# More descriptor room for GpSimd's indirect transfers, and two one-column buffers given up for it

## The chip, the cores and the metric

The kernel runs on one core of a Trainium2 chip. The metric is device time in microseconds (us) of one execution.
## The reference

One transformer layer on x of 1 x 2048 x 256, all in float32:

```python
x = x + layernorm(attention(layernorm(x)))   # 16 heads of 128, weights = 4-bit codes * block scales
x = x + layernorm(moe(layernorm(x)))
# moe: 8 experts, the two best of each token, weights from a softmax over the logits
combine = top-2 of softmax(x @ Wr), normalised
h = silu(x @ Wg[e]) * (x @ Wu[e]);  y = sum over e of combine[e] * (h @ Wd[e])
```

## The kernel before

Attention takes the first 1850 us. It works in 128 steps (`HALVES`: 16 heads of 8 slices of 256 queries), and every engine follows an order written out by hand. Values that need full precision are split into a high and a low part, so that each product is three matmuls (`product3`, lines 620 to 624).

The expert stage follows, and the change touches it. The 2048 tokens are 16 tiles of 128 rows, in two parts of 8 (`PART_TILES`). Each part is handled so:

1. PE turns the normed rows (`turn_rows`) and computes the router's logits (`route`, lines 842 to 857). DVE picks each token's two experts and works out the row that the token gets in a table sorted by expert (`shift_logits` to `rows_of`); the last step writes `row` (line 1756), an int32 index per token and choice. `seat_experts` then writes `expert_i` (line 1767), the expert of each seat. A seat is 128 rows of the table for one expert; part 0 and part 1 have 23 seats each (`SEATS`), 46 in all (`NS`).
2. POOL's `send(u)` (lines 587 to 596) scatters the tiles into the table `x_rows[u]` in DRAM: two indirect DMAs for each tile, one per choice, 16 for a part, each of 128 rows of 1 KB. All 16 of a part count on one semaphore, `x_sent[u]`.
3. SP's `load_seat` (lines 446 to 453) waits at seat 0 and at seat 23 until all 16 scatters of that part have landed, and loads each seat into one of four `xg` buffers. Before seat j it waits until seat j - 4 has been turned.
4. PE handles the seats in one order: `turn_h(n - 2)`, `turn_x(n + 1)`, `gate_up(n)`, `down(n - 3)` (lines 969 to 979). Its matmuls take the expert's weights at an address from a register; `expert_of` (lines 895 to 903) loads the register from `expert_i`. Seats 0 to 10 have theirs loaded ahead of part 1's rows; those of seats 11 to 22 are loaded in one run of 12 between `route(1)` and `turn_x(0)` (lines 965 to 968). ACT and DVE split the results (`seat_hi`, `seat_lo`, `gate`, `hidden`, `hidden_hi`, `hidden_lo`), and ACT empties the down product (`seat_out`, line 1276). The two turned tiles are signalled by `xg_t` (for ACT and SP) and `h_t` (for ACT).
5. `store_seat` writes each result to `y_rows[u]`; POOL's `fetch(t)` (lines 598 to 608) gathers each token's two rows by indirect DMA once the part's stores have landed, into four `yg` buffers with one semaphore each, and ACT and DVE weigh, add, norm and add the residual.

POOL's order in this stage is `down_lo`, `send(0)`, `send(1)`, `fetch(0..15)`. `send(1)` waits for part 1's `row`, which DVE computes while the first seats run.

`zero` (line 78) is one column of zeros, a bias operand for ACT in `scale_row` and `weigh` (lines 1123 and 1283); `warm` (line 85) takes the result of one square root whose only use is to have ACT load that table early (line 1190). `zeros` (128 x 256) is the source with which SP clears `x_rows` (line 434), and `wr_raw` holds the router's weights until POOL has split them at the start (lines 487 to 491).

Of the kernel before, what the change touches and what calls it, by code (L numbers as in the profile page):

```python
# [8 lines left out]
def sandwich_layer(nc, x, wq, sq, bq, wk, sk, bk, wv, sv, bv, wo, so, bo, wr, wg, wu, wd, out):  # L9
# [6 lines left out]
    f32, f32r = mybir.dt.float32, mybir.dt.float32r  # L16
    ALU, ACT, AX = mybir.AluOpType, mybir.ActivationFunctionType, mybir.AxisListType

    P = 128
# [26 lines left out]
    BATCHES = [(0, 8), (8, 4), (12, 4)]  # L46
    DVE_FROM = [6, 4]
    SEATS = [2 * n + E - 1 for _, n in PART_TILES]
    FIRST_SEAT = [sum(SEATS[:u]) for u in range(PARTS)]
    NS = sum(SEATS)  # L50
# [16 lines left out]
    with ctx:  # L67
        ctx.enter_context(nc.allow_non_contiguous_dma(reason="per-head bias columns"))

        def sem(name):  # L70
            return ctx.enter_context(nc.semaphore(name))

        def sb(name, shape, dt, stack=ctx):
            return stack.enter_context(nc.sbuf_tensor(name, shape, dt))

        ident = sb("ident", [P, P], f32)
        zero = sb("zero", [P, 1], f32)
        xT_hi = sb("xT_hi", [P, DC, S], f32r)
        xT_lo = sb("xT_lo", [P, DC, S], f32r)  # L80
        acc = sb("acc", [P, TT, D], f32)
        stats = sb("stats", [P, TT, 6], f32)
        mv = sb("mv", [P, TT, 2], f32)
        std = sb("std", [P, TT], f32)
        warm = sb("warm", [P, 1], f32)
        base = sb("base", [P, TT], f32)
        zeros = sb("zeros", [P, D], f32)
        wr_raw = sb("wr_raw", [P, DC, E], f32)
        wr_both = sb("wr_both", [P, DC, 2, E], f32r)
        rstd = sb("rstd", [P, TT], f32)  # L90
        shifted = sb("shifted", [P, TT], f32)
# [144 lines left out]
        sm = {n: sem(n) for n in names}  # L236
# [46 lines left out]
        def live(w):  # L283

            return 0 <= w < HALVES
# [29 lines left out]
        def bias_head(n):  # L315

            h, s = divmod(n, NH)
            if s == 3 and h == H - 2:
                return H - 2
            return (H - 1 if h == H - 2 else h) if s == 5 and 0 <= h < H - 1 else None  # L320
# [157 lines left out]

        @block.gpsimd
        def _(pool):  # L480
            pool.memset(zero[:, :], 0.0).then_inc(sm["ident_set"], 1)
            pool.memset(ident[:, :], 0.0).then_inc(sm["ident_set"], 1)
            pool.wait_ge(sm["ident_set"], 2)
            pool.affine_select(out=ident[:, :], in_=ident[:, :], compare_op=ALU.not_equal, fill=1.0,
                               base=0, pattern=[[-1, P]], channel_multiplier=1).then_inc(sm["ident_ready"], 1)

# [45 lines left out]
            for k, h in (("q", 0), ("v", 0), ("v", 1)):  # L532
                weights(k, h, first_codes[f"{k}{h}"], first_scales[f"{k}{h}"])

            pool.memset(zeros[:, :], 0.0).then_inc(sm["zeros_set"], 1)

            def constants():

# [444 lines left out]
        def _(act):  # L983
# [38 lines left out]
            def exps(w, r, g):  # L1022

                if not live(w):
                    return
                s = w % NH
                wait(act, "shift_ready", RH * w + r + 1)

                if r == 0 and g == 0:
                    wait(act, pT_loaded[s % 2], LOADS * (w // 2))  # L1030
                    if w == 0:
                        act.wait_ge(w_ready["q"], 1)
                        act.wait_ge(w_ready["v"], 2)
                out = blocks(s, g)[:, :, :, r, :].rearrange("p j t q -> p t j q")
                src = ring_of("s", w, NG2 * r + g).rearrange("p (t j q) -> p t j q", t=GT, j=Q4)
                if w == LAST:
                    out, src = natural(w)[:, r, g, :], ring_of("s", w, NG2 * r + g)
                nc.scalar.activation(out, src, ACT.Exp, bias=shift[:, s % SLOTS, r:r + 1],  # L1038
                                     scale=SCALE, accum_out=sums[:, s % SLOTS, r, g:g + 1])\
                    .then_inc(sm["p_ready"], 1)  # L1040

            def probs_hi(w, p):

                if not live(w):
                    return
                s, g, t = w % NH, p // GP, 2 * (p % GP)
                if p == 0 and w != LAST:
                    wait(act, pT_loaded[s % 2], LOADS * (w // 2 + 1))

                wait(act, "pv_done", PAIRS_KT * w + p - RING + 1)  # L1050
                if w == LAST:
                    wait(act, "last_turned", p // 2 + 1)
                    nc.scalar.activation(pT_hi[:, p, :], turned_pair(p), ACT.Copy).then_inc(sm["p_hi_done"], 1)
                    return
                nc.scalar.activation(pT_hi[:, p, :].rearrange("p (i n) -> p i n", i=Q4),  # L1055
                                     pT[:, s % 2, :, g, t:t + 2, :].rearrange("p i t q -> p i (t q)"),
                                     ACT.Copy).then_inc(sm["p_hi_done"], 1)

            def out_hi(w):

                if not live(w):
                    return
                s = w % NH
                wait(act, "pv_done", PAIRS_KT * (w + 1))

                wait(act, "oproj_ready", w)
                if w == LAST:
                    nc.scalar.activation(oT_hi[:, :], ps_a[:, s % 2, 0:HQ], ACT.Copy).then_inc(sm["out_hi"], 1)
                    return
                nc.scalar.activation(oT_hi[:, :].rearrange("p (r i q) -> p i r q", r=RH, i=Q4),  # L1070
                                     ps_a[:, s % 2, 0:HQ].rearrange("p (i r q) -> p i r q", r=RH, i=Q4), ACT.Copy)\
                    .then_inc(sm["out_hi"], 1)

            def q_hi(w):

                if not live(w):
                    return
                h, s = divmod(w, NH)
                wait(act, "q_ready", w + 1)
                if bias_head(w - 2) is not None:  # L1080
                    wait(act, "vb_ready", bias_head(w - 2) + 1)
                nc.scalar.activation(qT_hi[:, s % 2, :], ps_a[:, (s + 1) % 2, 0:HQ], ACT.Identity,
                                     bias=bias_all["q"][:, h:h + 1]).then_inc(sm["q_hi"], 1)

            def k_hi(h, b):
                wait(act, "k_ready", 2 * h + b + 1)
                cols = slice(b * HALF, (b + 1) * HALF)
                nc.scalar.activation(kT_hi[:, cols], ring_of("k", h, b), ACT.Identity,  # L1088
                                     bias=bias_all["k"][:, h:h + 1]).then_inc(sm["k_hi"], 1)

            def value_hi(pair, u):
                wait(act, "v_ready", VU * pair + u + 1)
                wait(act, "pv_done", PAIRS_KT * (2 * NH * pair - 1) + VT // 2 * (u + 1))
                nc.scalar.activation(v_hi[:, :, u * VT:(u + 1) * VT, :].rearrange("p e a d -> p a e d"),
                                     ring_of("v", pair, u).rearrange("p (a e d) -> p a e d", a=VT, e=2), ACT.Copy)\
                    .then_inc(sm["v_hi_done"], 1)

            def bias_hi(h):
                wait(act, "vb_ready", h)
                nc.scalar.activation(vb_hi[:, :], ident[:, :], ACT.Identity, bias=bias_all["v"][:, h:h + 1], scale=0.0)\  # L1100
                    .then_inc(sm["vb_hi_done"], 1)
# [58 lines left out]
            for n in range(-1, HALVES):  # L1160
                h, s = divmod(n, NH)
                inner, new_pair = live(n), live(n) and h % 2 == 0
                if n < 0:
                    q_hi(0)
                if bias_head(n + 1) is not None:
                    bias_hi(bias_head(n + 1))
                if new_pair and s == 3:
                    value_hi(h // 2, 2)
                probs_hi(n - 2, 1)
                exps(n, 0, 0)  # L1170
                if new_pair and s == 3:
                    value_hi(h // 2, 3)
                probs_hi(n - 2, 2)
                exps(n, 0, 1)
                if n >= 0:
                    q_hi(n + 1)
                probs_hi(n - 2, 3)
                probs_hi(n - 2, 4)
                probs_hi(n - 2, 5)
                probs_hi(n - 2, 6)  # L1180
                exps(n, 1, 0)
                exps(n, 1, 1)
                if new_pair and s in (1, 2):
                    value_hi(h // 2, s - 1)
                out_hi(n - 3)
                if s == NH - 1 and h + 1 < H:
                    k_hi(h + 1, 0)
                probs_hi(n - 2, 7)
                if n == LAST:
                    nc.scalar.activation(warm[:, :], zero[:, :], ACT.Sqrt).then_inc(sm["warm_done"], 1)  # L1190
                probs_hi(n - 1, 0)
                if s == NH - 1 and h + 1 < H:
                    k_hi(h + 1, 1)
# [739 lines left out]
```

## Time and profile before

| | |
|---|---|
| median of 3 runs | 2086.07 us (2084.23 to 2086.74) |
| the profiled execution | 2085.8 us |
| its span, first to last instruction | 2084.1 us |
| outside the span | 1.7 us |
| PE busy in the span | 1971.1 us, 95% |
| expert stage, from `send(0)` to the end | 1876.8 to 2084.1 us |

Sum what a change does inside the span; the 1.7 us around it stay. PE's share is an average: the attention is bound by PE, and the expert stage, which holds all indirect transfers, has stretches in which PE waits. The views with times are those to read for them: the chain of work that ended last, followed back from the end, the timelines of single engines, and the instructions of one line. Times in them are us from the span's start.

### The profile page before, as it was taken

Reading aid. Unit: us, or ns where it says so; the run is one execution under the profiler, and the core shown is the slowest. Engines: PE = TensorE matmul, PEld = TensorE weight load, DVE = VectorE, ACT = ScalarE, POOL = GpSimd, SP = SyncE. Lnnn points to the kernel's source line nnn. Section 1 sums busy time; section 2 is a strip of 40 time slices with the busy share of each in tenths; the row PEclk is TensorE's granted clock in tenths of the full one; section 3 lists DMA queues with packets and bytes.
Section 4 is the critical chain, followed back from the end, with each engine's and each line's share of the span. In section 5 each row is a group of like instructions: output and inputs, shape, how many; then the busy total and the mean of one; then the engine's idle time right before and its main releaser. Section 6 shows DMA issues by size and latency. Waiting matters only on the chain.

```text
span 2084.1 us, 33186 instructions
## 1 busy us (share of the span) xinstructions
PE 1971.1 (95%) x10902; PEld 1703.5 (82%) x10902; DVE 1750.8 (84%) x2706; ACT 1418.9 (68%) x2686; POOL 1528.5 (73%) x1317
## 2 busy tenths in 40 slices
PE   7999999999999999999999999999999999976882
PEld 5888888888888888888888888888888888865772
DVE  6889889998989888988999898988898888975344
ACT  4777767776777767776777677776777677763444
POOL 2679778887779777977888777977797787974222
PEclk9999999999999999999999999999999999987886
DMA  4667767786678667775777666766677576832343
GB/s 98 159 156 185 177 142 177 172 192 150 165 163 190 158 151 163 179 162 136 163 165 175 147 152 156 179 151 144 155 177 167 135 165 147 210 92 92 115 127 104
DMA packets 173040, 322.66 MB, mean 155 GB/s; under 512 B 47686, under 2 KB 105798, under 8 KB 172870
## 3 DMA queue, kind: packets, MB, share of 16 engines
q1 hardware_dynamic: 169798, 312.15, 64.0%
q0 software_dynamic: 3072, 8.39, 1.3%
q8 instruction: 89, 1.46, 0.3%
q14 instruction: 81, 0.66, 0.1%
HBM read 35.68 MB, written 18.35 MB: 26 GB/s over the span
## 4 chain that ended last, share of the span: by engine, by line
PE 82%; SPq 4%; POOL 3%; ACT 3%; DVE 3%; issue 2%; DMA 1%; another core or an unknown queue 1%; POOLq 0%; ACTq 0%
PE ps_a L750 20%; PE ps_s L622 14%; PE ps_s L624 13%; PE ps_s L623 13%; PE ps_a L751 10%; PE ps_a L622 3%; SPq L396 3%; PE ps_a L624 3%; PE ps_a L623 3%; POOL pT_both L519 2%; ACT probs L1038 1%; DVE part_max L1394 1%; POOL x_rows L595 1%; PE ps_s L928 1%
## 5 line engine op out<-in xcount | busy, mean ns | idle before, releaser
L519 POOL TENSOR_TENSOR pT_both<-pT,pT_both 128x512 fp32r<-128x512 f32 x1016 | 1291.2, 1301 | 339.9 <-ACT pT_both L1055 337.8
L1038 ACT ACTIVATE probs<-ps_s,shift 128x1024 f32<-128x1024 f32 x512 | 566.6, 1110 | 275.6 <-DVE shift L1403 275.5
L750 PE MATMUL ps_a<-pT_both,v_both 128*128 128x512 f32 x2048 | 744.3, 397 | 0.7 <-POOL pT_both L519 0.5
L1055 ACT ACTIVATE pT_both<-pT 128x512 fp32r<-128x512 f32 x1016 | 606.7, 629 | 162.8 <-DMA pT<-probs 128.8
L1419 DVE STREAM_TRANSPOSE probs<-probs 128x1024 f32<-128x1024 f32 x508 | 614.5, 1229 | 56.8 <-ACT probs L1038 55.9
L1394 DVE TENSOR_REDUCE part_max<-ps_s 128x1 f32<-128x1024 f32 x512 | 612.5, 1215 | 20.6 <-PE ps_s L624 19.0
L751 PE MATMUL ps_a<-pT_both,v_both 128*128 128x256 f32 x2048 | 573.9, 280 | 0.0
L750 PEld LDWEIGHTS ps_a<-pT_both,v_both 128*128 128x128 f32 x2048 | 385.5, 188 | 86.1 <-POOL pT_both L519 1.3
L622 PE MATMUL ps_s<-kT_hi,qT_hi 128*128 128x512 f32 x1024 | 406.6, 397 | 11.7 <-ACT probs L1038 8.6
L623 PE MATMUL ps_s<-kT_lo,qT_hi 128*128 128x512 f32 x1024 | 403.3, 394 | 0.0
L624 PE MATMUL ps_s<-kT_hi,qT_lo 128*128 128x512 f32 x1024 | 401.9, 392 | 0.0
L751 PEld LDWEIGHTS ps_a<-pT_both,v_both 128*128 128x128 f32 x2048 | 386.7, 189 | 15.9
L622 PEld LDWEIGHTS ps_s<-kT_hi,qT_hi 128*128 128x128 f32 x1024 | 192.4, 188 | 56.9 <-ACT probs L1038 10.4
L624 PEld LDWEIGHTS ps_s<-kT_hi,qT_lo 128*128 128x128 f32 x1024 | 192.6, 188 | 45.1
L623 PEld LDWEIGHTS ps_s<-kT_lo,qT_hi 128*128 128x128 f32 x1024 | 192.8, 188 | 22.5
L1476 DVE SCALAR_TENSOR_TENSOR acc<-ps_a,rinv,acc 128x256 f32<-128x256 f32 x240 | 104.0, 475 | 2.4 <-PE ps_a L624 2.2
L606 POOL DMA_INDIRECT yg<-y_rows,row x32 | 31.1, 972 | 96.7 <-DMA y_rows<-y_sb 74.8
L1038 ACT ACTIVATION_READ_ACCUMULATOR probs<-ps_s,shift 128x1 f32 x512 | 98.8, 193 | 0.0
L1491 DVE SCALAR_TENSOR_TENSOR kT_lo<-ps_s,bias_k,kT_hi 128x1024 fp32r<-128x1024 f32 x32 | 41.1, 1284 | 43.7 <-ACT kT_hi L1088 43.7
L622 PE MATMUL ps_a<-w_o_hi,oT_hi 128*128 128x256 f32 x256 | 73.6, 288 | 1.2 <-DVE oT_lo L1439 1.2
L622 PE MATMUL ps_a<-xT_hi,w_q_hi 128*128 128x256 f32 x256 | 72.4, 283 | 0.0
L623 PE MATMUL ps_a<-w_o_lo,oT_hi 128*128 128x256 f32 x256 | 72.2, 282 | 0.0
(202 smaller groups left out, 2596.6 us busy)
## 6 DMA issues: line engine op xcount, KB each, us to landing
pT<-probs SPq DMA_DIRECT2D x2032, 128.0 KB, 2.3
x_rows<-zeros SPq DMA_DIRECT2D x46, 128.0 KB, 2.1
xg<-x_rows SPq DMA_DIRECT2D x46, 128.0 KB
y_rows<-y_sb SPq DMA_DIRECT2D x46, 128.0 KB
pT<-in_L_attn_x SPq DMA_DIRECT2D x4, 512.0 KB, 5.6
codes<-in_L_attn_wk_codes SPq DMA_DIRECT2D x16, 128.0 KB, 2.4
scales<-in_L_attn_wk_scales SPq DMA_DIRECT2D x64, 32.0 KB, 2.9
codes<-in_L_attn_wo_codes SPq DMA_DIRECT2D x16, 128.0 KB, 2.3
```

What stands on the lines that cost most here:

```text
L396: sp.dma_start(dst, src).then_inc(pT_loaded[s % 2], 16)
L519: pool.tensor_tensor(pT_lo[:, p, :].rearrange("p (i n) -> p i n", i=Q4), pT[:, s % 2, :, g, t:t + 2, :].rearrange("p i t q -> p i (t q)"), ...
L622: nc.tensor.matmul(dst, lhs_hi, rhs_hi, start=first, stop=False)
L623: nc.tensor.matmul(dst, lhs_hi, rhs_lo, start=False, stop=False)
L624: return nc.tensor.matmul(dst, lhs_lo, rhs_hi, start=False, stop=last)
L750: nc.tensor.matmul(out_both, v_hi[:, h % 2, k, :], move, start=k == 0, stop=False)
L751: last = nc.tensor.matmul(out, v_lo[:, h % 2, k, :], move[:, 0], start=False, stop=k == KT - 1)
L1038: nc.scalar.activation(out, src, ACT.Exp, bias=shift[:, s % SLOTS, r:r + 1], scale=SCALE, accum_out=sums[:, s % SLOTS, r, g:g + 1])\
L1055: nc.scalar.activation(pT_hi[:, p, :].rearrange("p (i n) -> p i n", i=Q4), pT[:, s % 2, :, g, t:t + 2, :].rearrange("p i t q -> p i (t q)" ...
L1394: V.tensor_reduce(part_max[:, s % SLOTS, r, g:g + 1], ring_of("s", w, NG2 * r + g), AX.X, ALU.max)\
L1419: V.transpose(tile, tile).then_inc(sm["p_turned"], 1)
L1476: ins = V.scalar_tensor_tensor(acc[:, t, :], part, scale, acc[:, t, :], ALU.mult, ALU.add)
```

## The change

The scratch area for indirect transfers grows from 1024 to 4096 bytes per partition. To pay for it, `zero` and `warm` lose their own buffers: `zero` becomes the first column of `zeros`, `warm` the first column of `wr_raw`. The fill of `zeros` moves from behind the first weights to the very start of POOL's program, in the place of the fill of `zero`, and the wait ahead of the `affine_select` counts one fill in place of two. Each buffer takes a multiple of 32 bytes of a partition, so 64 are given back and those above the two lie 3008 bytes higher.

```diff
-        zero = sb("zero", [P, 1], f32)
...
-        warm = sb("warm", [P, 1], f32)
         base = sb("base", [P, TT], f32)
         zeros = sb("zeros", [P, D], f32)
+        zero = zeros[:, 0:1]
         wr_raw = sb("wr_raw", [P, DC, E], f32)
+        warm = wr_raw[:, 0, 0:1]
...
-            pool.memset(zero[:, :], 0.0).then_inc(sm["ident_set"], 1)
+            pool.memset(zeros[:, :], 0.0).then_inc(sm["zeros_set"], 1)
             pool.memset(ident[:, :], 0.0).then_inc(sm["ident_set"], 1)
-            pool.wait_ge(sm["ident_set"], 2)
+            pool.wait_ge(sm["ident_set"], 1)
...
-            pool.memset(zeros[:, :], 0.0).then_inc(sm["zeros_set"], 1)
...
-                    nc.scalar.activation(warm[:, :], zero[:, :], ACT.Sqrt).then_inc(sm["warm_done"], 1)
+                    nc.scalar.activation(warm, zero[:, :], ACT.Sqrt).then_inc(sm["warm_done"], 1)
...
-    nc = bacc.Bacc("TRN2", target_bir_lowering=False, num_devices=1, dynamic_dma_scratch_size=1024)
+    nc = bacc.Bacc("TRN2", target_bir_lowering=False, num_devices=1, dynamic_dma_scratch_size=4096)
```

## Rows read from the trace of the kernel before

**Rows 1.** The page: its first line.
```profile
span 2084.1 us, 33186 instructions
```

**Rows 2.** POOL's timeline: start us, us, operation, [idle before <-releaser].
```profile
1876.79 1.20 POOL L595 DMA_INDIRECT x_rows<-acc,row  x1 [8.30 <-issue]
...
1888.18 0.97 POOL L595 DMA_INDIRECT x_rows<-acc,row  x1 [2.03 <-issue]
...
1898.88 0.97 POOL L595 DMA_INDIRECT x_rows<-acc,row  x1 [2.04 <-issue]
...
1922.49 0.96 POOL L595 DMA_INDIRECT x_rows<-acc,row  x1 [20.86 <-DVE row L1756]
...
1933.10 0.96 POOL L595 DMA_INDIRECT x_rows<-acc,row  x1 [2.04 <-issue]
```

**Rows 3.** POOL's and ACT's timelines while part 0's results are gathered.
```profile
1987.57 0.98 POOL L606 DMA_INDIRECT yg<-y_rows,row  x1 [41.63 <-DMA y_rows<-y_sb]
...
1996.40 0.95 POOL L606 DMA_INDIRECT yg<-y_rows,row  x1 [0.30 <-issue]
...
1997.66 0.32 ACT L1260 ACTIVATE silu_g<-ps_a 128x176 f32<-128x176 f32 x1 [3.64 <-remote]
```

**Rows 4.** The chain that ended last, in order: start us, us, what.
```profile
1886.14 2.03 issue
...
1896.84 2.04 issue
...
1900.16 3.01 DMA x_rows<-acc,row
1903.19 2.06 DMA xg<-x_rows
1905.29 0.70 PE ps_s L891 x2
```

**Rows 5.** Line 903, 1890 to 1906: ns min/median/max, first and last start.
```profile
L903 PEldq TENSOR_LOAD <-expert_i x12: 295/301/552, 1895.7 to 1903.1; - x12
...
L903 PEldq SEQ_ASSERT  x12: 18/18/18, 1896.3 to 1903.7; - x12
```

**Rows 6.** DVE's timeline, its work for part 1's routing.
```profile
1898.37 0.29 DVE L1666 TENSOR_REDUCE logits<-ps_s 128x64 f32<-128x128 f32 x1 [3.04 <-PE ps_s L855]
...
1903.12 0.28 DVE L1707 TENSOR_TENSOR which<-rank,count 128x128 f32<-128x128 f32 x1
```

**Rows 7.** What SP's queue waited for from 1895 on: us, times, longest.
```profile
SPq L453 <- DMA x_rows<-acc,row: 63.7, 1, 63.7
```

**Rows 8.** The timeline of PE and ACT during part 1's scatters.
```profile
1924.34 0.41 PE L622 MATMUL ps_a<-gu_hi,xs_hi 128*128 x1
...
1926.74 0.41 PE L622 MATMUL ps_a<-gu_hi,xs_hi 128*128 x1
...
1931.13 0.38 ACT L1268 ACTIVATE hs_hi<-ps_s 88x256 fp32r<-88x256 f32 x1 [3.95 <-remote]
...
1935.62 0.64 PE L622 MATMUL ps_a<-gu_hi,xs_hi 128*128 x1
...
1939.25 0.40 PE L622 MATMUL ps_a<-gu_hi,xs_hi 128*128 x1
...
1946.26 0.64 PE L622 MATMUL ps_a<-gu_hi,xs_hi 128*128 x1
...
1949.71 0.41 PE L622 MATMUL ps_a<-gu_hi,xs_hi 128*128 x1
```

**Rows 9.** The start: POOL's fills, PE's warm-up and its first real work.
```profile
0.80 0.10 POOL L481 MEMSET zero<- 128x1 f32 x1 [0.29 <-POOLq L1922]
...
1.62 7.21 PE L639 MATMUL ps_a<-ident 128*128 128x128 f32 x40 [1.62 <-POOL ident L484]
...
10.90 1.09 PE L633 MATMUL ps_s<-ident,pT 128*128 128x128 f32 x8 [2.07 <-ACT pT L1001]
...
21.61 0.31 POOL L535 MEMSET zeros<- 128x256 f32 x1
```

## The prediction

> **What bounds the kernel now.** I read the chain of waits first, from the end back to the start of the expert stage, because only what stands in it can shorten the run. Around POOL's first 16 scatters it runs through POOL alone: send by send, then the landing of the last scatter, the load of seat 0 (1903.19 to 1905.25), and PE's first turn of a seat at 1905.29 [rows 4]. Among the sends it has two pieces called "issue" of 2.03 and 2.04 us [rows 4]. POOL's timeline shows where they lie: ahead of the 8th and the 15th send, where all others of this run follow after 0.30 us, as in the gathers [rows 2, 3]. In part 1 the same stands ahead of the 8th and the 15th of its sends (the 24th of all, at 1933.10, and the 31st likewise) [rows 2]. So after every seven sends in a row comes one wait. The count began anew after the pause of 20.86 us ahead of the 17th send [rows 2]: the 17th to the 23rd went freely, the 24th waited. That is the picture of a room that holds seven transfers and is full when the eighth comes. Each wait ends about 2.05 us after POOL is through with the send before it, which is also what the load of seat 0 took to land [rows 4]: POOL waits for the newest of the seven, not for the oldest, which was sent over 10 us before. The gathers, up to eight in a row, never waited (0.30 us ahead of the eighth) [rows 3]. They differ in that each pair has its own semaphore, where the 16 scatters of a part share one; so the room of an old pair can be taken back alone.
>
> **The room, four times as large.** By scale it holds 28 transfers. The waits at sends 8, 15 and 24 find no reason any more. The first send that could meet a full room is the 29th, the 13th of part 1, and what it has to take back first are part 0's, which had all landed by 1903.19 [rows 4]. I take all four waits as gone; should one in part 1 stay, it costs 1.74 us of POOL's time with nobody behind it, as shown below. Each wait is 2.03 or 2.04 us less the usual 0.30, so the two of part 0 give 1.73 + 1.74 = 3.47 us: the last scatter lands at 1899.7, and seat 0 is there at 1905.25 - 3.47 = 1901.78.
>
> **What is late next.** PE doesn't stand idle until then. Between `route(1)` and `turn_x(0)` its queue loads 12 experts' numbers, one after the other: the first load starts at 1895.7, the last assert at 1903.7, which is 8.0 / 12 = 0.67 us for each [rows 5]. They depend on nothing that moves, so `turn_x(0)` can't start before 1903.72. I put it at 1903.75: a gain of 1905.29 - 1903.75 = **1.54 us**, and the remaining 1.93 us of the 3.47 are hidden. The other candidate is DVE, which must be through with `choose(1)` before `seat_lo(0)`: its last piece starts at 1903.12 and takes 0.28, end 1903.40 [rows 6]. The seat's low part would be wanted some 1.1 us after the turn starts (two turns 0.70 [rows 4], one ACT copy 0.38 as in [rows 8]), at 1904.8. DVE is free by then. The bounds of this term are 0 (the loads are slowed and end where the data came before) and 3.47 (they end early). The Trainium skill, page "DMA: Bandwidth & Descriptors", section "Latency and other measured facts", gives a floor of some 600 ns for such a register load. The trace has 0.67 us for one with its two register operations; by the page's figure, estimated, 12 would end at 1895.7 + 7.2 = 1902.9, and the term would be 2.4 us. The row decides.
>
> **Part 1's scatters** end 3.47 us earlier too, but SP's queue waited for a scatter once only, at seat 0 [rows 7]; seat 23, the first of part 1, is loaded long after they have landed. The gathers wait for stores of results, not for sends. Price of the direct effect: 0.
>
> **The indirect effect on the seats.** While POOL issues, PE's signals reach ACT late: in part 1's run ACT sat idle 3.95 us with its input turned, put down to "remote", which no engine of one core can be [rows 8]. The first matmul of `gate_up` came every 1926.74 - 1924.34 = 2.40 us before, and then at 1935.62, 1939.25, 1946.26 and 1949.71 [rows 8]. Four seats in 22.97 us, where 9.6 would do: 13.4 us are lost during and just behind part 1's scatters, 8.9 - 2.4 = 6.5 on the first of them and 7.0 - 2.4 = 4.6 on the third. The 13.4 us don't come from the waits for room as such, since ACT also lost 3.64 us while POOL gathered without a wait [rows 3]. After the change POOL issues 16 sends in one run of about 16 x 1.27 = 20.3 us (0.97 + 0.30 for one [rows 2]) in place of 7, 7 and 2 with two breaks. I take the loss as unchanged, 0, between two ends: it falls by the third seat's 4.6 us plus the seat behind it, 3.45 - 2.40 = 1.05, so by 5.65; or it grows by 7.2 us (rival 2). That is the widest term, and no row settles it.
>
> **The edits with one answer.** The fill of 256 columns takes 0.31 us where that of one took 0.10 [rows 9], and stands ahead of `ident`: PE's warm-up starts and ends up to 0.21 us later, at 9.04 in place of 8.83, and PE's first real work starts at 10.90 on ACT's norm [rows 9]. Price 0, hidden by that; 0.21 us if the cover were gone. The old fill at 21.61 goes [rows 9]; it frees 0.31 us of POOL that nobody waits for, at most a gain of the same size. `warm` and `zero` at other addresses take the same instructions and no new wait, on ACT's queue too. All other buffers shift by 3008 or 3040 bytes; no row prices that, and I bound it by 0.2 us either way, the size of the fill's edit.
>
> **Sum.** 2084.1 - 1.54 = 2082.6 us of span, with 1.7 us outside it 2084.3 for a profiled execution [rows 1]. That execution (2085.8) lay 0.27 us below the median of 2086.07, so the prediction in terms of the median is 2086.07 - 1.54 = **2084.5 us**.
>
> **The rivals.**
>
> 1. *The loads don't bind.* If PE's loads end earlier once POOL disturbs them less, the whole 3.47 us come through, less what DVE takes: its 1903.40 against 1901.78 + 1.1 = 1902.9 costs 0.5, so 3.0 us: 2083.1. Against it: their end is in the trace [rows 5], with POOL idle ahead of it for 2.04 us.
> 2. *One long run starves the seats (slower).* Place: PE's signals to ACT and SP in part 1's run. The breaks of 2 us are what lets them through: ACT's late piece started at 1931.13, when POOL had just finished its seventh send and was waiting until 1933.10 [rows 2, 8]. Without a break the seat in flight would stand still until the 16 sends are through, some 20.3 us after the start. PE began three seats between 1926.74 and 1946.26 [rows 8]; all three, 3 x 2.4 = 7.2 us of work, would come behind the run. Time: 2084.5 + 7.2 = 2091.7. A milder form has the loss grow with the time that POOL issues, with 14 sends x 1.27 = 17.8 us before, 13.4 x 20.3 / 17.8 = 15.3, so +1.9: 2086.4. It decides from the point where more than 1.54 us are added. Against it: gathers without a break let ACT go on too, if late.
> 3. *One long run has one stall.* If each run stalls once, the second goes: 2084.5 - 5.65 = 2078.9. For it: the loss came once in each of the two long runs [rows 8].
> 4. *The waits aren't for room.* They could be POOL held up by DVE's work, and then stay whatever the room: 2086.1. But DVE was idle for 3.04 us until 1898.37, through most of the second gap, which began at 1896.84 [rows 4, 6], and the strict count of seven speaks for room. That such a hold exists is what the Trainium skill says (page "SBUF — State Buffer", section "SBUF: two separate sides": GpSimd can't write descriptors while VectorE has the port that they share); here the trace doesn't show it.
>
> **How the numbers follow.** The forecast (1.54 us, the seats' loss as before or within 2 us of it) 0.45; rival 1 0.10; rival 2 0.22, of which 0.12 above 2090.2; rival 3 0.15; rival 4 0.08. The range from 2079.0 to 2090.0 takes in rival 3 but for half of its lower side, and rival 2 up to three quarters of its price; what is left out is some 0.2. A measurement tells about 0.2%, 4.2 us, from no change. Faster than 2081.9 is rival 3 and a little of rival 1 and of the forecast with a smaller loss: 0.20. Slower than 2090.2: 0.12. The rest, 0.68, is within 0.2%.
>
> **What would show it.** In POOL's timeline, 0.30 us ahead of every scatter but the 1st and 17th. Seat 0's load landing some 1.9 us before PE's turn of it, and that turn starting right behind the last assert of line 903, about 8 us after the first load. The spacing of `gate_up` from the 8th seat on tells rivals 2 and 3. The prediction is wrong if the gaps of 2 us stay, if the turn starts well before or after that assert, or if the seats during part 1's scatters lose much more or less than 13 us.

## The result

In the sitting in which the change was judged (a sitting is one chip with the kernel before timed beside the others), the kernel before has a median of 2084.09 us and the changed kernel 2088.89 us: a ratio of 1.0024, 95% interval 1.0014 to 1.0034, so **slower by 4.8 us** where 1.5 us faster was predicted. The profiled execution has 2090.6 us of span. Later sittings were of two kinds, and this is the larger finding: where the kernel before has 2085 us the changed one has 1.0027 (1.0016 to 1.0038); where it has 2063 us, the changed one has **0.9975** (0.9966 to 0.9985), faster by 5.3 us. Ratios compare executions in the fast state; one of 11 of the kernel called `spaced` below took 6843 us and stands in none of them.

The waits for room are gone, as said. POOL's timeline of the changed kernel, with the lines that answer to those of [rows 2], has 0.30 us ahead of the 8th send (1883.33) and of the last; all that follow between them are alike:

```profile
1883.33 0.96 POOL L594 DMA_INDIRECT x_rows<-acc,row  x1 [0.30 <-issue]
...
1893.44 0.96 POOL L594 DMA_INDIRECT x_rows<-acc,row  x1 [0.30 <-issue]
```

The chain of waits (start, us, what) shows what came in their place. Before, it ran through POOL's sends and the load of seat 0 [rows 4]. Now it doesn't touch them:

```profile
1890.34 0.60 ACT xT_hi L1148
1890.93 2.19 another core or an unknown queue
...
1893.14 0.60 ACT xT_hi L1148
1893.74 2.92 another core or an unknown queue
...
1896.68 0.60 ACT xT_hi L1148
...
1898.65 0.38 PE ps_s L852
...
1902.02 0.21 PE ps_s L854
1902.23 4.26 issue
1906.49 0.70 PE ps_s L890 x2
```

PE has turned part 1's rows, but the signals of two of the four turns reach ACT 2.19 and 2.92 us after ACT is ready. One core has no other core to wait for; this is the piece that [rows 8] called "remote". The 32 matmuls of `route(1)` behind them (lines 852 and 854) stand 0.21 us apart, at a granted clock of 0.50; from 1893.80 to 1897.60 in the profile of before they ran at 0.89, in 3.85 us in place of 7.27. The row of line 902's loads shows how the delay goes on: they start three microseconds later than in [rows 5], 5.8 us later if counted from the first send, and PE's turn of seat 0 (1906.49) stands right behind the last assert.

```profile
L902 PEldq TENSOR_LOAD <-expert_i x12: 295/301/307, 1898.7 to 1905.9; - x12
...
L902 PEldq SEQ_ASSERT  x12: 18/18/18, 1899.3 to 1906.4; - x12
```

In part 1's run the same thing is larger. ACT's timeline has idle times of 3.99, 7.12 and 5.36 us; PE's has the seats:

```profile
1932.29 0.38 ACT L1267 ACTIVATE hs_hi<-ps_s 88x256 fp32r<-88x256 f32 x1 [3.99 <-remote]
...
1940.75 0.32 ACT L1259 ACTIVATE silu_g<-ps_a 128x176 f32<-128x176 f32 x1 [7.12 <-remote]
1946.43 0.38 ACT L1267 ACTIVATE hs_hi<-ps_s 88x256 fp32r<-88x256 f32 x1 [5.36 <-remote]
```

```profile
1927.94 0.41 PE L621 MATMUL ps_a<-gu_hi,xs_hi 128*128 x1
...
1936.03 0.64 PE L621 MATMUL ps_a<-gu_hi,xs_hi 128*128 x1
...
1949.74 0.64 PE L621 MATMUL ps_a<-gu_hi,xs_hi 128*128 x1
```

Between the ninth `gate_up` and the eleventh lie 21.8 us; in [rows 8] two steps from 1926.74 take 12.5. I use four numbers of each profiled execution from here on: the **first send**; **gate 0**, from the first send to the first matmul of `gate_up`; **early loss**, from `gate_up` of seat 0 to that of seat 22, less 22 x 2.40; and **late loss**, the same for the 23 steps behind it, in which part 0's results are gathered. The two profiles of the judged sitting:

| kernel | span | first send | gate 0 | early loss | late loss |
|---|---|---|---|---|---|
| before | 2084.1 | 1876.79 | 30.5 | 13.5 | 13.1 |
| changed | 2090.6 | 1873.99 | 34.5 | 17.5 | 14.1 |

So 4.0 us are lost ahead of the seats, 4.0 in part 1's run, 1.0 in the gathers and 0.3 behind the last seat; and 2.8 come back from ahead of the first send, which nothing in the prediction allowed.

### The profile page after: what moved, and what is told of

The parts are those of the page before. It is cut to its first block, busy times and chain, and to the rows that moved or that the text cites. A ratio compares the mean times of both kernels' runs of the same rounds, so it can differ in the third digit from the quotient of the medians.

```text
span 2090.6 us, 33185 instructions
## 1 busy us (share of the span) xinstructions
PE 1968.6 (94%) x10902; PEld 1700.9 (81%) x10902; DVE 1752.0 (84%) x2706; ACT 1417.8 (68%) x2686; POOL 1524.8 (73%) x1316
## 4 chain that ended last, share of the span: by engine, by line
PE 75%; SPq 6%; POOL 5%; DVE 5%; ACT 4%; issue 2%; DMA 2%; another core or an unknown queue 1%; POOLq 0%; ACTq 0%; DVEq 0%
PE ps_a L749 18%; PE ps_s L621 13%; PE ps_s L622 12%; PE ps_s L623 12%; PE ps_a L750 9%; SPq L396 6%; POOL pT_both L519 4%; PE ps_a L621 3%; PE ps_a L623 3%; PE ps_a L622 3%; ACT probs L1037 2%; DVE part_max L1393 1%; DMA pT<-probs 1%; DVE probs L1418 1%
## 5 line engine op out<-in xcount | busy, mean ns | idle before, releaser
L621 PE MATMUL ps_s<-kT_hi,qT_hi 128*128 128x512 f32 x1024 | 406.6, 397 | 11.7 <-ACT probs L1037 8.6
L605 POOL DMA_INDIRECT yg<-y_rows,row x32 | 30.4, 951 | 106.2 <-DMA y_rows<-y_sb 84.1
```

The lines of the kernel that those rows point to most:

```text
L621: nc.tensor.matmul(dst, lhs_hi, rhs_hi, start=first, stop=False)
```

## The experiments

Three theories. **A**: PE's signals are late while POOL issues indirect transfers without a pause; the waits for room were pauses. **B**: the traffic of the scattered rows holds them up. **C**: the small edits cost it.

**The edits alone.** The room back at 1024, all other edits kept.

```
-dynamic_dma_scratch_size=4096
+dynamic_dma_scratch_size=1024
```

> The changed kernel with its room put back to 1024 bytes; the edits to the zero column, the warm-up scratch and the start of POOL stay. Theory (the longer runs of scatters hold up PE's signals; part 0: turn_x(0) came 32.50 us after the first send where it came 28.50 us after it before, part 1: the four slowed steps of the seats 26.9 us where they were 23.0): the waits of 2.03 us are back at the 8th, 15th, 24th and 31st send, turn_x(0) 28.5 us behind the first send, and the time is that of before, ratio 0.999 to 1.001. Rival (the small edits cost it: the attention moved, or the code): no wait changes that, 1.002 or more. Third: the profile of after began its first send 2.80 us earlier than before; if that comes from the edits and not from scatter of the runs, this one is at 0.9987.

Measured: 0.9988 (0.9977 to 0.9999), before at 2084.36. Gate 0 is 30.5, the early loss 11.9, as before. C falls with its sign turned: the edits *win* about 2.5 us (0.2 to 4.8 by the interval). The profiles show where. `v_proj` issues groups of 24 matmuls of 128x256 on w_v. First and last of one group, before:

```profile
515.04 0.28 PE L622 MATMUL ps_s<-w_v_hi,xT_hi 128*128 128x256 f32 x1
...
517.76 0.28 PE L624 MATMUL ps_s<-w_v_hi,xT_lo 128*128 128x256 f32 x1
```

and in the changed kernel:

```profile
514.03 0.28 PE L621 MATMUL ps_s<-w_v_hi,xT_hi 128*128 128x256 f32 x1
...
516.64 0.28 PE L623 MATMUL ps_s<-w_v_hi,xT_lo 128*128 128x256 f32 x1
```

2.72 us against 2.61 for 23 steps: 118.3 and 113.5 ns for one. In two profiles of before all whole groups of the 32 have 117.8 to 118.7. In three profiles of kernels with the edits the first of every four has 117.4 to 117.8 and the other three 113.5 to 113.9, but for the second and third of all, which lie between. The granted clock is 1.00 around both groups shown. The three products have 256 such matmuls each, so 768 / 24 = 32 groups; three quarters of them x 0.11 = some **2.6 us**. No instruction changed; the addresses did. That this is the cause is argued, and which buffer's address counts wasn't tried.

**Which of the waits mattered.** Both kernels have the room of 28. POOL stops ahead of a part's 8th and 15th send until those out have landed, in part 0 alone or in part 1 alone.

```
 for k in range(2):
+    sent = 2 * (t - PART_TILES[u][0]) + k
+    if u in (0,) and sent in (7, 14):      # (1,) in the other
+        pool.wait_ge(x_sent[u], 16 * sent)
```

> The changed kernel, with its room of 28 transfers, and in part 0 alone POOL waits for the transfers that are out before the 8th and the 15th send; part 1's run stays unbroken. Theory: it is the stop in POOL's run that lets PE's signals through, so turn_x(0) is again 28.5 us (27.0 to 29.5) behind the first send and the 4.0 us of part 0 come back, while part 1 keeps its loss of about 3.9 us: ratio about 1.0005 to 1.001 against before (after minus 4.0 is 2084.9, with the scatter of the profile 2085 to 2087). Rival (the size of the room matters itself, or the loss sits in part 1 alone): 1.0024 stays, 2089.

> The changed kernel, with its room of 28 transfers, and in part 1 alone POOL waits for the transfers that are out before its 8th and 15th send; part 0's run stays unbroken. Theory: turn_x(0) stays 32.5 us behind the first send (31 to 33), the gate_up steps from the ninth to the thirteenth take 23.0 us again instead of 26.9, ratio about 1.0005 to 1.001 (2085 to 2087). Rival (all the loss is in part 0): 1.0024 stays, 2089. Should both this and the kernel with part 0's waits give the 4.9 us nearly alone, then neither loss simply adds up.

Measured, in the sitting of the kernel with the edits alone (0.9988) and against before: part 0's waits 1.0025 (1.0012 to 1.0038), gate 0 30.8, early loss 18.2. Part 1's waits 1.0001 (0.9991 to 1.0010), gate 0 31.2, early loss 9.3. I had expected each to bring half. ACT's timeline with part 1's waits has pieces put down to "remote" only up to the first pause (POOL's second run starts at 1929.11):

```profile
1926.64 0.38 ACT L1267 ACTIVATE hs_hi<-ps_s 88x256 fp32r<-88x256 f32 x1 [3.25 <-remote]
1927.37 0.38 ACT L1251 ACTIVATE xs_hi<-ps_s 128x256 fp32r<-128x256 f32 x1 [0.34 <-remote]
1928.88 0.32 ACT L1259 ACTIVATE silu_g<-ps_a 128x176 f32<-128x176 f32 x1 [0.85 <-remote]
```

The seats behind it are still slowed, with steps of 3.5, 3.8 and 4.8 us, but the piece of 7.12 us is gone. Most of the change's loss sits in part 1's run, and a wait in that run had kept it small. The larger room by itself isn't what makes the early loss: it is 28 here too, with 9.3 us.

**Pauses that wait for seats.** In part 1 each pair of sends waits for ACT's signal of a seat.

```
+if u == 1:
+    pool.wait_ge(sm["xs_hi_done"], 8 + 3 * (t - PART_TILES[1][0]) // 2)
```

> The changed kernel; part 0's run unbroken, and in part 1 each pair of sends waits for seats: pair i (0 to 7) for the 8 + 3i/2-th signal of xs_hi (ACT), so that two sends of 2.53 us together come every 3.6 us with about 1 us free between them, and the last one about seat 18, ahead of seat 20 at which SP first asks for them. Theory (a signal of PE comes late only while POOL issues one indirect transfer straight after another, and only some us into such a run, 2 to 5): the seats keep their 2.40 us through part 1's sends, the 13 us that before lost there and the 17 of after vanish: 2089 - 17 = 2072, down to half that gain if pairs still disturb, 2080. Rival 1 (each indirect transfer holds up signals, however far apart): the same loss spread over more seats, 2089. Rival 2 (part 1's seats then wait for their rows at seat 23): the idle time shows ahead of PE's turn of x at seat 23 on a DMA, 2080 to 2092.

Measured: 0.9996 (0.9985 to 1.0007), early loss 10.7; a miss. The waits of two neighbouring seats let four sends go in a row, four times, and each run of four, 4.7 us long, cost 2.1 to 3.3 us, with ACT idle on "remote" for 1.01, 2.61, 2.61 and 3.50 us.

**The next sitting: nothing is late.** Four kernels were meant to measure the length of the run and the cause.

```
room14, the room alone:
+dynamic_dma_scratch_size=2048
single1, ahead of each send of part 1:
+pool.wait_ge(sm["xs_hi_done"], 8 + 2 * (t - PART_TILES[1][0]) + k)
pair1, ahead of each pair of part 1:
+pool.wait_ge(sm["xs_hi_done"], 8 + 2 * (t - PART_TILES[1][0]))
plain1, in place of each send of part 1 (it leaves out the sorting by expert:
the rows lie in the order of the tiles, so part 1's results are others):
+pool.dma_start(x_rows[1][n * P:(n + 1) * P, :], acc[:, t, :]).then_inc(x_sent[u], 16)
```

> The changed kernel with a room of 2048 bytes (14 transfers by the count seen at 1024). POOL should stop 2.04 us only ahead of the 15th and the 31st send. Theory as it stands after the first four kernels (the loss sits in part 1's run and grows with the length of the unbroken run; seats 0 to 22 lost 9.3 to 13.5 us against a pace of 2.40 us where part 1's sends went 7, 7, 2 and 17.5 to 18.2 us where they went 16 in a row): a run of 14 loses nearly as much as one of 16, 15 to 18 us, ratio 1.001 to 1.002. Rival (only what a run has beyond some 10 sends is dear, or a few microseconds of stop anywhere free the signals): 10 to 13 us, ratio about 0.999 to 1.000.

> The changed kernel; part 0's run unbroken, part 1's sends one for each seat: send i (0 to 15) waits for the (8 + i)-th signal of xs_hi (ACT), so that 1.26 us of issue stand in every 2.40 us, with about 1.1 us free after each. In the kernel with waits for each pair the pairs of neighbouring seats had joined to four runs of four, and each of these cost 2.1 to 3.3 us. Theory A (PE's signal is late only when POOL issues without a pause): no seat is slowed by the sends, seats 8 to 19 at 2.40 us, loss over seats 0 to 22 about 1 to 2 us from other causes. Theory B (each indirect transfer or each start of a run costs something): 16 times 0.6 us or more, 10 us and up. In either case the last send goes at seat 22 only, and seat 23 waits for its rows, 3 to 7 us by the DMA rows (landing 3.0, load 2.1): ratio 0.998 by A, 1.002 by B.

> The changed kernel; part 0's run unbroken, part 1's sends two for every second seat: pair i (0 to 7) waits for the (8 + 2i)-th signal of xs_hi (ACT), 2.53 us of issue in every 4.80 us, with 2.2 us free behind each pair. Theory A (late only in an unbroken run, from its second or third microsecond on): a run of two is over before a signal is held up, or one in some is: loss over seats 0 to 22 at most 4 us. Theory B (every start of a run costs 2 to 3 us, as each run of four did): 8 x 2.5 = 20 us. Seat 23 waits for its rows as with single sends, 2 to 6 us: ratio 0.998 to 0.999 by A, over 1.004 by B.

> The changed kernel, but part 1's 16 scatters are 16 ordinary transfers of the same 128 rows of 1 KB to fixed places of the same array, issued by POOL at the same point (the rows then lie in the order of the tiles and not by expert: that part of the result is another). Theory (it is POOL's own work on an indirect transfer, 0.96 us of it for each, that holds up PE's signals): seats 8 to 12 keep 2.40 us, the loss over seats 0 to 22 falls from 17.5 to 1 or 2 us, the span to 2090.6 - 16 = 2074 or less. Rival (it is the traffic of the scattered rows in the 16 DMA queues, the signal waiting behind it): the same bytes go in less time, so the loss stays above 5 us and may come at once and longer.

Before was at 2061.44, 23 us faster than until then. Ratios 0.9977 (0.9966 to 0.9987), 0.9993 (0.9984 to 1.0002), 0.9996 (0.9987 to 1.0005); plain1 had one execution, 2058.9. Early losses 0.4, 3.5, 2.8 and 0.4, late losses 1.2 to 2.6. Even a run of 14 sends lost nothing, so these four don't tell A from B at all. They do say that the room counts as the prediction had it: with 2048 bytes POOL stops 2.12 us ahead of the 15th send and 2.43 ahead of the 31st. The 3 us of single1 and pair1 are seat 23 waiting for its rows, 3.04 us on "DMA xg<-x_rows" in single1.

**Again, beside both kernels.**

> The kernel before once more, for its profile beside those of this call. Until here the kernel before had 2084 us in two sittings, with seats slowed by 12 to 13 us during part 1's scatters and again during part 0's gathers, and 2061 us in a third, in which no kernel showed that loss (seats 0 to 22 lost 0.4 us, the others 1.2 to 2.6). Theory: PE's late signals belong to the sitting (the chip or its state) and are the 23 us between the two. So this profile has either 2058 to 2063 us and every gate_up step of seats 3 to 42 at 2.40 us, or 2080 to 2088 us and a loss of 12 to 14 us twice. Rival: the kernel before shows the losses in either sitting and the 23 us are elsewhere (attention).

> The changed kernel once more. In a sitting of 2061 us: no signal of PE is late, so only the path up to seat 0 changes: turn_x(0) 26.9 to 27.4 us behind the first send where before has 28.5, and part 1's sends end 4 us earlier, which nobody waits for: ratio 0.998 to 0.9995. In a sitting of 2084 us: 1.0024 again, with 4 us lost in part 1's run and up to 4 us in part 0's. Rival (the change costs its 4.8 us everywhere): 1.0024 in both.

> The changed kernel with part 1's 16 scatters as ordinary transfers of the same bytes to fixed places (that part of the result is another). In a sitting of 2084 us: if POOL's work on indirect transfers holds the signals up, seats 0 to 22 lose 1 to 2 us where the changed kernel loses 17.5; if the traffic does, more than 5 us. In a sitting of 2061 us there is nothing to take away, 0.4 us as in the first look.

> The changed kernel with part 1's sends one for each seat from the ninth on. In a sitting of 2084 us: if only unbroken runs hold signals up, seats 8 to 19 stay at 2.40 us and the only loss is at seats 21 and 22, which wait for rows (3.1 us in the other sitting): 2089 - 17.5 + 3.5 = 2075, ratio 0.9955; if every transfer costs something, 10 us lost and more, ratio 1.000 to 1.003. In a sitting of 2061 us: 0.9993 as measured there.

Before was at 2085.24, and the losses were back: 11.7 and 13.4 in its own profile, 17.6 and 12.8 in the changed kernel's (1.0027, gate 0 32.6). Here A and B part. plain1 (2075.28 us, one execution) moves the same 16 x 128 KB over the same seats, issued in 8.62 us, and PE keeps its pace:

```profile
1923.62 8.62 POOL L596 DMA_DIRECT2D x_rows<-acc  x16 [26.47 <-DVE row L1755]
```

```profile
1925.43 0.41 PE L621 MATMUL ps_a<-gu_hi,xs_hi 128*128 x1
...
1927.82 0.41 PE L621 MATMUL ps_a<-gu_hi,xs_hi 128*128 x1
...
1930.22 0.41 PE L621 MATMUL ps_a<-gu_hi,xs_hi 128*128 x1
...
1932.61 0.41 PE L621 MATMUL ps_a<-gu_hi,xs_hi 128*128 x1
```

Early loss 0.1. The traffic is denser than in the changed kernel, not thinner: the DMA engines move 228 GB/s on average from 1923 to 1940, against 126 there from 1923 to 1946. Nor is the run too short to show anything, since four indirect transfers in 4.7 us were enough. B falls, on one execution of this kernel, and the next one bears it out. Single sends (A's test) have **0.9958** (0.9945 to 0.9972), 8.3 us faster than before, with 16 indirect transfers as before but a pause behind each. Against the changed kernel of the same sitting (2090.72) that is 13.8 us, and the early losses differ by 14.1:

```profile
1925.41 0.96 POOL L596 DMA_INDIRECT x_rows<-acc,row  x1 [26.91 <-ACT xs_hi L1251]
1927.31 0.96 POOL L596 DMA_INDIRECT x_rows<-acc,row  x1 [0.95 <-ACT xs_hi L1251]
1930.19 0.96 POOL L596 DMA_INDIRECT x_rows<-acc,row  x1 [1.91 <-ACT xs_hi L1251]
```

No seat from the ninth to the twentieth is over 2.53 us, and the 3.5 us of early loss are the wait for seat 23's rows:

```profile
1965.64 0.69 PE L890 MATMUL ps_s<-ident,xg 128*128 128x128 f32 x2 [3.08 <-DMA xg<-x_rows]
```

Idle of 0.95 and 1.91 us in turn between two sends is enough, and POOL needs to await no landing. The same profile keeps its late loss, 16.3 us, in the gathers, which go 8 in a row.

**The gathers too, and the register loads.** `spaced` gives both parts pauses, with part 0's results weighed every 3/2 seats instead of 5/4; `loads` moves the twelve register loads into the loop over seats; `spaced_loads` does both.

```
spaced, ahead of send i of part 1, and of each gather of part 0:
+pool.wait_ge(sm["xs_hi_done"], 8 + 3 * i // 4)
+pool.wait_ge(sm["xs_hi_done"], 30 + 3 * (2 * t + k) // 4)
...
loads, ahead of turn_x(0), and behind gate_up(n):
-for j in range(SEATS[0] // 2, SEATS[0]):
-    expert_of(j)
...
+if n < SEATS[0] - SEATS[0] // 2:
+    expert_of(SEATS[0] // 2 + n)
```

> The changed kernel with room for its transfers in both places and a pause between them: in part 1 send i waits for the (8 + 3i/4)-th signal of xs_hi, so that the last goes at seat 18 and not 22, and part 0's gather g for the (30 + 3g/4)-th; the seats at which part 0's results are weighed lie 3/2 seats apart instead of 5/4. Theory (only unbroken runs hold PE's signals up), in a sitting of 2084 us: seats 0 to 22 lose 0.5 to 1 us (single sends 3.5, of which 3 to 4 were the wait for rows at seats 21 to 23), the rest loses 1 to 5 us instead of 13 to 16 during the gathers: 2077 - 3 - 11 = 2063, ratio 0.990. Rival (gathers hold up for another reason, or doubles of two in a row suffice): 8 to 14 us stay in the seats after 29, ratio 0.995. In a sitting of 2061 us: only the 3 us at seat 21 come back, 0.997 to 0.999.

> The kernel with spaced sends and gathers, and PE's twelve register loads for experts 11 to 22 stand in the loop over seats, one behind each of the first twelve gate_up, instead of ahead of turn_x(0). The prediction's step: once the waits for room are gone these loads end last ahead of turn_x(0). If so turn_x(0) comes nearer to the first send: in a sitting of 2061 us from 27.4 to about 26.0 (last landing and the load of xg: 20.4 + 3.0 + 2.1 = 25.5, and 0.4), ratio 0.0005 to 0.0007 below the kernel without this; in a sitting of 2084 us, where route(1) ends late, from 29.2 to 32.5 to 26 to 28.5, 3 to 4 us or 0.0015 to 0.002 lower. Rival (the loads are hidden, DMA or route(1) itself ends last): no difference of turn_x(0) over 0.3 us.

> The changed kernel with nothing but the twelve register loads moved into the loop over seats. Same theory: turn_x(0) 26 to 28.5 us behind the first send in a sitting of 2084 us (after: 32.5 and 30.6), the loss of 17.5 us in seats 0 to 22 stays: ratio 1.0024 - 0.0017 = 1.0007. In a sitting of 2061 us 26.0 instead of 27.4. Rival (loads hidden): 1.0024 to 1.0027 as after.

Before was at 2062.05. Ratios 0.9978 (0.9967 to 0.9989), 0.9987 (0.9978 to 0.9996), 0.9990 (0.9981 to 1.0000). The gathers' test had nothing to show here. Moving the loads brought no time that these show, though in `loads` PE turns seat 0 24.2 us behind the first send instead of 27 or so. PE's timeline says who is late next:

```profile
1899.15 0.36 PE L852 MATMUL ps_s<-wr_both,xT_hi 128*128 128x16 f32 x1
1899.37 0.35 PE L854 MATMUL ps_s<-wr_both,xT_lo 128*128 128x8 f32 x1
1899.62 0.69 PE L890 MATMUL ps_s<-ident,xg 128*128 128x128 f32 x2
1905.26 0.66 PE L890 MATMUL ps_s<-ident,xg 128*128 128x128 f32 x2 [4.95 <-DVE xs_lo L1790]
```

DVE is in `choose(1)` until 1904.7 and makes seat 0's low part only then. In this execution `route(1)` ended 3.1 us later behind the first send than in the profile of before, its matmuls 0.21 us apart: the granted clock is 0.50 throughout it, with PE busy all the time and no signal late. So DVE came late, and gate 0 is 30.2, as in `spaced` (30.2, clock 0.50 too). At the upper level moving the loads does show: `spaced_loads` (0.97) has a gate 0 of 27.0, `spaced_2` further down (0.91) 28.8. But its early loss is 1.3 in place of -0.4, with steps of 2.86 and 3.04 us behind the 11th and 12th `gate_up`, so nearly all of the 1.8 us is paid back inside the loop.

**The three side by side.**

> The kernel before a third time, for its profile beside those of this call. In a sitting of 2061 us: the first gate_up 30.0 to 30.5 us behind the first send (30.52 and 29.98 in the two sittings of 2084 us, since with the waits the last transfer sets it), no seat slowed by part 1's sends or by the gathers. In a sitting of 2084 us: the loss of 12 to 13.5 us twice.

> The changed kernel a third time. In a sitting of 2061 us, where no signal of PE was late: the first gate_up 29.4 us behind the first send (the three kernels with part 0's run unbroken, or broken at the 15th send alone, had 29.4 to 30.2) where before has 30.0 to 30.5, part 1's waits worth nothing, and the small edits 0 to 2.5 us (the kernel with those alone had 0.9988): ratio 0.998 to 0.9995, faster. In a sitting of 2084 us 1.0024 to 1.0027 as twice measured. Rival: the change costs its 4.9 us in either sitting, 1.0024.

> The kernel with spaced sends and gathers once more. In a sitting of 2084 us: single sends had 0.9958 with 3.5 us lost by seat 22, of which 3 waiting for rows, and 16.3 us in the seats behind it, during the gathers. If the pause between transfers is what frees PE's signals, here too both losses fall to 1 to 5 us together: 0.9958 x 2085 = 2076, less 13: 2063, ratio 0.990. If runs of up to four, as these waits give them, still cost 2 to 3 us each (as they did in the kernel with waits for each pair), about 8 runs: 2080, 0.998. In a sitting of 2061 us 0.9978 as measured.

Before was at 2063.04. The changed kernel has 0.9975 (0.9966 to 0.9985), spaced 0.9982 (0.9973 to 0.9992), so the pauses are worth nothing where no signal is late. The chain of the changed kernel is the one that the prediction drew: landing, load of seat 0, then 2.72 us of PE's own:

```profile
1894.42 2.40 DMA x_rows<-acc,row
...
1896.84 1.97 DMA xg<-x_rows
1898.81 2.72 issue
1901.53 0.70 PE ps_s L890 x2
```

```profile
L902 PEldq SEQ_ASSERT  x12: 18/18/18, 1894.3 to 1901.5; - x12
```

PE's turn at 1901.53 stands right behind the last assert. In the chain of before, of this sitting, the two waits of the first run are 2.03 and 2.04 us and the turn follows the load:

```profile
1903.03 3.43 DMA x_rows<-acc,row
1906.47 1.88 DMA xg<-x_rows
1908.40 0.70 PE ps_s L891 x2
```

All profiles that carry the argument, in the two kinds of sitting:

| sitting, kernel | sends of part 0; 1 | first send | gate 0 | early loss | late loss |
|---|---|---|---|---|---|
| 2084, before | 7,7,2; 7,7,2 | 1876.79 | 30.5 | 13.5 | 13.1 |
| 2085, before | 7,7,2; 7,7,2 | 1878.14 | 30.0 | 11.7 | 13.4 |
| 2084, edits alone | 7,7,2; 7,7,2 | 1873.85 | 30.5 | 11.9 | 12.3 |
| 2084, part 0 waits | 7,7,2; 16 | 1879.92 | 30.8 | 18.2 | 11.5 |
| 2084, part 1 waits | 16; 7,7,2 | 1872.25 | 31.2 | 9.3 | 14.2 |
| 2084, pairs by seats | 16; 4,4,4,4 | 1874.96 | 31.9 | 10.7 | 14.1 |
| 2084, changed | 16; 16 | 1873.99 | 34.5 | 17.5 | 14.1 |
| 2085, changed | 16; 16 | 1873.54 | 32.6 | 17.6 | 12.8 |
| 2085, plain | 16; none indirect | 1876.38 | 32.6 | 0.1 | 14.2 |
| 2085, single | 16; singles | 1877.76 | 31.9 | 3.5 | 16.3 |
| 2063, before | 7,7,2; 7,7,2 | 1879.80 | 30.6 | 0.2 | 1.5 |
| 2063, changed | 16; 16 | 1874.69 | 28.9 | 0.3 | 1.3 |
| 2063, spaced | 16; 3,1,3,1,3,1,4 | 1873.33 | 28.8 | -0.4 | -0.3 |

## Why the prediction was wrong

**The room: right.** All four waits went, and half the new room stops POOL after 14 sends. Rival 4 is out. The rule of the Trainium skill named beside it (page "SBUF — State Buffer", section "SBUF: two separate sides") shows in no run here.

**What is late next, the 1.54 us: right in mechanism and nearly in size, where signals are on time.** Gate 0 fell from 30.63 to 28.86 us, 1.77 us, between the two profiles of 2063, with PE's loads last. These two had `route(1)` at a granted clock of 0.94 and 0.99. In the kernels of those sittings that had it at 0.50 (`room14`, `single1`, `pair1`, `spaced`) gate 0 is 29.4 to 30.2, a gain of 0.5 to 1.2 us only; that level of PE's clock no term of the prediction had. That DVE isn't late held too, but by little: its last piece of `choose(1)` starts 25.96 us behind the first send and PE's turn 26.84. At the lower clock it is late, and taking the loads away then won nothing. Twelve loads took 8.0 us in [rows 5] and 7.8 here (1893.7 to 1901.5), so the row was the better guide than the 0.6 us that the Trainium skill gives (page "DMA: Bandwidth & Descriptors", section "Latency and other measured facts"). Rival 1 is out.

**The small edits at 0, bounded by 0.2 us: the bound failed.** "No row prices that" was true, and the bound was taken from an unrelated edit. They are worth 2.6 us of gain by the pitch of `v_proj`, and 2.5 by the measured times (0.2 to 4.8). Three of before's first sends average 1878.2 and the changed kernel's three 1874.1, which is more, but first sends of kernels with the same code ahead of them lie anywhere from 1871.7 to 1879.9.

**The indirect effect on the seats at 0, the step that failed.** The prediction saw the late signals, called this the widest term, and took the middle. In the sittings of 2084 the early loss is 11.6 us on average where part 1's sends are broken after seven (13.5, 11.7, 11.9, 9.3) and 17.8 where they aren't (17.5, 17.6, 18.2): **+6.2 us**, near rival 2's 7.2 and not its mild 1.9; rival 3 has the opposite sign and is out. Its reason for the 0 was that ACT went on, if late, in gathers without a break; those runs are of 8, not of 16. Rival 2 had the place and nearly the size, but not quite the picture: PE didn't stand still until the last send, one `gate_up` came at 1936.03 in the middle of the run, and the next 6.1 us behind its end (1943.63). The prediction had also written down the fact that decided: that ACT's late piece started just when POOL paused.

**A place that it did not look at.** The prediction said of the twelve loads that "they depend on nothing that moves". They stand in PE's queue behind `route(1)`, and that waits for part 1's rows to be turned and split, by signals of PE to ACT. The rows are turned about 15 to 17 us behind the first send. Before, that fell shortly behind the first wait for room. With no wait POOL has been issuing for 15 us, and the turns' signals come late: gate 0 is 31.2 to 34.5 us, 32.5 on average of six profiles, against 30.0 to 30.8, average 30.4, of four with the waits. That is **+2.0 us** in place of -1.54, with a wide scatter. All six have a "remote" wait of 2.2 us or more ahead of ACT's `xT_hi`, and none of the four has one, nor any kernel of 2061 to 2063. Part of the 2.0 is PE's clock: the six have `route(1)` at 0.50 to 0.69, and that level alone went with 0.6 to 1.4 us more of gate 0 where no signal was late. How much of it the late signals brought on isn't shown, since it also came without them.

**The sum as it should have been.** In a sitting of 2084: -2.6 + 2.0 + 6.2 = +5.6 us, measured +4.8 and +5.5. In one of 2063: -2.6 - 1.8 = -4.4, measured -5.3 (-3.1 to -7.0 by the interval). That it is faster there owes more to the edits, which the prediction priced at nothing, than to the term that it foresaw. One part of the prediction is right in each kind of sitting, and the trace that it was read from was of the kind in which the other part is larger.

**Still open.** What makes a sitting the one or the other. The five whose chip is on record were on five chips (2084 and 2085 us on chips 0 and 9; 2061, 2062 and 2063 us on chips 1, 11 and 10), so a property of the chip and a state of the moment can't be told apart. The profiles of the kernel before differ by 21.7 us of span, and early and late loss together are 26.6 us in the one and 1.7 in the other. By what way a signal of PE is held up isn't shown; only that POOL's issue of indirect transfers in an unbroken run does it. That a semaphore for each pair is why the gathers never stopped for room wasn't tried. That spacing the gathers frees the late loss is unproven: that kernel was timed only in sittings where there was none. No version beats both kernels in both: single sends do at 2085 (0.9958 against 1.0027), and at 2061 to 2063 they have 0.9993 where the changed kernel has 0.9975.

## What to carry to other kernels

A wait that looks like pure loss may be the only pause of its engine, and others may live on it: before taking it away, ask in the trace what gets through while it lasts. Where the trace shows PE's signals late beside a long run of indirect transfers, issue them one by one, with a wait on the loop's own progress; where it shows none, the pauses win nothing (0.9982 with them, 0.9975 without, in one sitting). When a buffer is added or dropped, compare the pitch of the matmuls with the trace of before, even where no instruction changed.

## What was unexpected of the hardware

- PE's signals to ACT came up to 7.12 us late while POOL issued indirect transfers back to back (0.96 us of issue each, 0.30 between), and not in a sitting of the same kind with a pause behind each (0.95 us or more, once 0.47), nor with ordinary transfers of the same bytes. In three sittings of 2061 to 2063 us no signal was late; in three of 2084 to 2085 seats were slowed beside the runs of four and more.
- Matmuls of 128x256 with a weight load each followed each other in 118.3 ns with one placement of the buffers and in 113.5 with another, 2.6 us in this kernel. The granted clock was 1.00 in both; the placement as the cause is argued.
- The same 32 small matmuls of `route(1)` took 3.5 to 3.9 us with PE's clock mostly at the upper level and 6.6 at the lower, and the level differed between profiles of like code: 0.89 and 0.50 in two profiles of the kernel before.
- With the room of 1024 bytes POOL's wait ahead of the 8th send of part 1 was 2.04 us in one kind of sitting [rows 2] and 4.56 us in the other, where the seats ran at full pace beside it:

```profile
1938.61 0.96 POOL L595 DMA_INDIRECT x_rows<-acc,row  x1 [4.56 <-issue]
```
